# Scaling W1 behind node tiles 23 to 33, and gating edge step 0 before step 1's rows are fetched

## What is computed

```python
x = layernorm(x + L0(x))      # mean over neighbours, three 256-wide products, a gate for each node
# L1, for each of 4 heads:
feats  = relu(x @ W1 + b1) @ W2 + b2
hid    = relu(concat(feats[row], feats[col], elem) @ A1 + ab1)
w      = exp(leaky_relu(hid @ A2 + ab2) - max)
pooled = segment_sum(w * feats[col], row) / segment_sum(w, row)
x = layernorm(x + pooled)
```

## Time and profile before

| | us |
|---|---|
| median of 3 runs | 2942.45 (2941.87 to 2944.29) |
| the profiled execution, its own time | 2944.66 |
| its span, first to last instruction | 2942.9 |
| first block, until | about 27 |
| merged block, until | about 1031 |
| edge block, until | about 2630 |
| mean granted clock of PE | 0.973 |

### The profile page before, as it was taken

How to read it: one execution, slowest core, us unless ns; L and a number is a source line. 1 busy time by engine, 2 the same in 40 slices (tenths; PEclk the granted TensorE clock), 3 DMA queues, 4 the chain that set the end, 5 groups by cost and what they waited for, 6 DMA issues and landing times. The chain is left out here.

```text
span 2942.9 us, 52181 instructions
## 1 busy us (share of the span) xinstructions
PE 2697.9 (92%) x13617; PEld 1554.7 (53%) x13617; DVE 2329.0 (79%) x7668; ACT 1851.3 (63%) x3839; POOL 1582.4 (54%) x1491
## 2 busy tenths in 40 slices
PE   4789889999999959999999999999999999976774
PEld 2455556666666525555555555555555555543442
DVE  8777775655565668888888888888888888878996
ACT  2344445555555437777777777777777777757885
POOL 0476717676666375455455454454554554405776
PEclk8799999999999979999999999999999999999998
DMA  9999995565555478777777787777777777647994
GB/s 339 304 301 314 306 308 182 187 192 180 182 189 189 143 182 218 215 223 214 213 227 214 213 221 216 215 218 217 219 217 212 226 213 212 193 118 241 278 278 154
DMA packets 544632, 653.46 MB, mean 222 GB/s; under 512 B 244302, under 2 KB 451850, under 8 KB 544518
## 3 DMA queue, kind: packets, MB, share of 16 engines
q1 hardware_dynamic: 468486, 440.38, 51.6%
q0 software_dynamic: 69472, 208.99, 22.7%
q10 hardware_dynamic: 6560, 2.84, 0.4%
HBM read 315.65 MB, written 299.10 MB: 209 GB/s over the span
## 5 line engine op out<-in xcount | busy, mean ns | idle before, releaser
L942 PE MATMUL bank<-w_node,xT 128*128 128x384 f32 x1564 | 568.5, 501 | 47.2 <-ACT bank L576 46.9
L1219 ACT ACTIVATE hidT<-bank,b1c 128x512 f32<-128x512 f32 x490 | 336.8, 687 | 414.5 <-PE bank L1509 340.7
L1128 POOL TENSOR_TENSOR u_hc<-u_hc 128x1536 f32<-128x1536 f32 x98 | 270.2, 2757 | 551.0 <-issue 429.0
L1509 PE MATMUL bank<-xh,w1h 128*128 128x512 f16 x1568 | 469.8, 381 | 23.1 <-DMA xh<-eh 15.7
L1509 PE MATMUL bank<-xl,w1h 128*128 128x512 f16 x1568 | 468.2, 380 | 0.0
L1509 PE MATMUL bank<-xh,w1l 128*128 128x512 f16 x1568 | 468.2, 380 | 0.0
L942 PEld LDWEIGHTS bank<-w_node,xT 128*128 128x128 f32 x1564 | 291.4, 195 | 227.7 <-ACT bank L576 61.6
L576 ACT ACTIVATE bank<-bias_all 128x512 f32<-128x512 f32 x391 | 234.3, 599 | 267.4 <-DVE H L680 266.2
L1525 PE MATMUL bank<-hidT,w2f 128*64 128x256 f32 x3136 | 360.1, 382 | 0.8 <-ACT hidT L1219 0.8
L1350 DVE STREAM_TRANSPOSE feat<-catT 32x256 f32<-32x256 f32 x784 | 342.5, 437 | 17.0 <-ACT catT L1228 2.4
L673 DVE SCALAR_TENSOR_TENSOR H<-bank,gates,X 128x256 f32<-128x256 f32 x391 | 187.2, 479 | 175.1 <-PE bank L942 172.5
(11 more groups left out here) (248 smaller groups left out, 4833.0 us busy)
## 6 DMA issues: line engine op xcount, KB each, us to landing
hc_tab<-H SPq DMA_DIRECT2D x78, 680.0 KB, 7.9
er<-edge_tab SPq DMA_DIRECT2D x98, 512.0 KB
X<-in_x SPq DMA_DIRECT2D x78, 640.0 KB, 4.8
h_row<-hc_tab SPq DMA_DIRECT2D x97, 512.0 KB
out_x<-o_row SPq DMA_DIRECT2D x97, 512.0 KB, 5.0
hc_tab<-zero_row SPq DMA_DIRECT2D x35, 1344.0 KB, 8.4
edge_tab<-u_x SPq DMA_DIRECT2D x98, 256.0 KB
edge_tab<-feat SPq DMA_DIRECT2D x98, 256.0 KB
```

Source lines behind the costliest of these rows:

```text
L942: ins = t_.matmul(p[:, 0:384], xT[t // 2 % XR][:, t % 2, c * P:(c + 1) * P], w_node[:, c, :], start=False, stop=c == 1, skip_group_check=True)
L1128: g.tensor_tensor(c, c, u_hc[s][:, :, MULT:MULT + 3].unsqueeze(3).to_broadcast([P, 4, 3, P]), ALU.mult).then_inc(u_scaled, 1)
L1219: a.activation(hidT[m][:, :], bank[2 + m % 2][:, :], ACT.Relu, bias=b1c[:, m:m + 1])\
L1509: ins = t_.matmul(bank[2 + m % 2][:, :], w[:, c, m * P:(m + 1) * P], xx[s][:, :, :].rearrange("p (k c) e -> p c k e", c=2)[:, c, :, :], st ...
```

## The change

The eleven pieces of `scale_w1` go into the merged block. Behind tile 22 PE turns W1 (now into banks 4 to 7), behind tile 28 it spreads the powers. On DVE piece k stands behind tile 23 + k: pieces 0 to 3 one bank's maxima and minima each, 4 the powers, 5 b1 and W2, 6 and 7 the product with W1 (half the columns each), 8 the cast, 9 and 10 the subtraction, now one half of 1,024 elements each. Their buffers and semaphores are made in the merged block. In the edge block `scale_w1`, the transposes and PE's wait for `rows_read` go. On POOL the order becomes fetch 0, gate 0, fetch 1, fetch 2, gate 1, fetch 3, gate 2, and so on.

```diff
@@ merged block @@
+        SCALE = 22
@@ DVE @@
+                def scale_w1(k):
+                    if k < 4:
+                        w1_extremes(k)
+                    elif k == 4:
+                        w1_powers()
+                    elif k == 5:
+                        w2_down()
+                    elif k < 8:
+                        w1_up(k - 6)
+                    elif k == 8:
+                        w1_high()
+                    else:
+                        w1_low(k - 9)
...
+                def w1_low(c):
+                    if c == 0:
+                        st.wait()
+                    st.done(v.tensor_tensor(w1l[:, c, :], w1f[:, c, :], w1h[:, c, :], ALU.subtract))
+                    if c:
+                        st.wait()
+                        dve.sem_inc(w1_scaled, 1)
...
+                    if 0 <= now - SCALE - 1 < 11:
+                        scale_w1(now - SCALE - 1)
@@ PE @@
+                def turn_w1():
+                    pe.wait_ge(edge_sem, pc[1])
...
+                    if now == SCALE:
+                        turn_w1()
+                    if now == SCALE + 6:
+                        turn_up()
@@ edge block, POOL @@
-                skewed(pool, US, GS, [(gate, 2), (fetch, 0)])
+                fetch(0, 0)
+                gate(0, 0)
+                fetch(1, 1)
+                skewed(pool, US, GS, [(gate_rest, 2), (fetch_rest, 0)])
@@ edge block, DVE @@
-                scale_w1()
@@ edge block, PE @@
                 open_scores(0)
-                for m in range(MB):
-                    for c in range(2):
-                        o = (2 * m + c) % 4 * P
-                        ins = t_.transpose(bank[2 + m // 2][:, o:o + P], w1f[:, c, m * P:(m + 1) * P], ident[:, :])
-                ins.then_inc(w_turned, 1)
-                pe.wait_ge(up_ready, 1)
...
-                pe.wait_ge(rows_read, 4)
                 open_scores(1)
```

More of the change, by code:

```diff
@@ L391, in build @@
         o_main = out[0:P * NT].rearrange("(p t) d -> p t d", p=P)
+        MB = 2 * HEADS
+        X_UP = float(1 << 11)
+        TOP = 13
+        w_most, w_least = tmp("w_most", [P, MB]), tmp("w_least", [P, MB])
+        w_pow, w_up = tmp("w_pow", [P, MB], I32), tmp("w_up", [P, MB], I32)
+        w_down = tmp("w_down", [P, MB])
+        w_turned, up_ready, up_rows, rows_read, w1_scaled = (sem(n) for n in (
+            "w1_turned w1_up_ready w1_up_rows w1_rows_read w1_scaled").split())
         PAIRS = ET // 2
@@ new lines, in w2_down @@
+                def w2_down():
+                    dve.wait_ge(edge_sem, pc[1])
+                    dve.sem_inc(dve_hop, 1)
+                    st.done(v.scalar_tensor_tensor(out=b1c[:, :], in0=b1c[:, :], scalar=X_UP,
+                                                   in1=w_up[:, :].bitcast(F32), op0=ALU.mult, op1=ALU.mult))
+                    st.done(v.tensor_tensor(w2f[:, :, :], w2f[:, :, :],
+                                            w_down[:, :].unsqueeze(2).to_broadcast([P, MB, FEAT]), ALU.mult))
@@ new lines, in w1_up, with w1_high @@
+                def w1_up(i):
+                    dve.wait_ge(up_rows, 1)
+                    sl = slice(i * 512, (i + 1) * 512)
+                    for c in range(2):
+                        st.done(v.tensor_tensor(w1f[:, c, sl], w1f[:, c, sl], bank[4 + i][:, :], ALU.mult))
+                def w1_high():
+                    st.wait()
+                    st.done(v.tensor_copy(w1h[:, :, :], w1f[:, :, :]))
+                def w1_low(c):
+                    if c == 0:
+                        st.wait()
+                    st.done(v.tensor_tensor(w1l[:, c, :], w1f[:, c, :], w1h[:, c, :], ALU.subtract))
+                    if c:
+                        st.wait()
+                        dve.sem_inc(w1_scaled, 1)
@@ L987, in sums, with turn_up @@
                         product_sum(2 * (p - LAG_P) + 1)
+                def turn_w1():
+                    pe.wait_ge(edge_sem, pc[1])
+                    for m in range(MB):
+                        for c in range(2):
+                            o = (2 * m + c) % 4 * P
+                            ins = t_.transpose(bank[4 + m // 2][:, o:o + P], w1f[:, c, m * P:(m + 1) * P],
+                                               ident[:, :])
+                    ins.then_inc(w_turned, 1)
+                def turn_up():
+                    pe.wait_ge(up_ready, 1)
+                    for m in range(MB):
+                        o = m % 4 * P
+                        ins = t_.transpose(bank[4 + m // 4][:, o:o + P],
+                                           w_up[:, m:m + 1].bitcast(F32).to_broadcast([P, P]), ident[:, :])
+                    ins.then_inc(up_rows, 1)
                 def carries():
@@ L1062, in build @@
         ACT_M, DVE_M = (0, 2, 4, 6, 7), (1, 3, 5)
[L1063 to L1070, removed]
         hidT = [tmp(f"hidT{m}", [P, 512]) for m in range(8)]
@@ L1133, in gate, with gate_rest, fetch_rest @@
                         .then_inc(u_gated, 1)
-                skewed(pool, US, GS, [(gate, 2), (fetch, 0)])
+                def gate_rest(u, s):
+                    if not isinstance(u, int) or u > 0:
+                        gate(u, s)
+                def fetch_rest(u, s):
+                    if not isinstance(u, int) or u > 1:
+                        fetch(u, s)
+                fetch(0, 0)
+                gate(0, 0)
+                fetch(1, 1)
+                skewed(pool, US, GS, [(gate_rest, 2), (fetch_rest, 0)])
             @block.sync
```

19 lines of the change are left out of this document (added).

## The result

| | before | after |
|---|---|---|
| median of the runs | 2943.32 (16 runs) | 2949.01 (16 runs) |
| lowest to highest | 2941.87 to 2945.25 | 2945.15 to 2951.70 |
| the profiled execution, its own time | 2944.66 | 2945.15 |
| its span | 2942.9 | 2943.4 |

What follows compares the result with a forecast made beforehand. DMA was taken to bound 130 to 440 us, PE the two long stretches after. A merged-block shift of +10.5 us, handed on, and -0.5 at the edge block's start gave +10.0: median 2952.5 us, range 2941 to 2961.

Steps and rivals of the forecast that it cites:

- The pieces on DVE: Merged block: the eleven pieces of scale_w1 cost DVE 13.1 us in sum (12.5 to 14).
- The rule on the cast: Piece 8 on DVE could wait for one indirect DMA's issue, making the sum 14 us instead of 13.1.
- Transposes of W1: PE at tile 22 of the merged block: 16 transposes put 2.0 us on the path.
- The second set: PE's 8 transposes behind tile 28, when DVE is the slower engine: 0 us on the path (bound 1).
- The landing: The store after tile 34 lands 8.7 to 9.7 us after issue, so the next half shifts +9.5 to +11.4, taken +10.5.
- Does the rest come back?: DMA-bound stretch after tile 34: no, the shift, taken as +10.5 us, is handed on to the end.
- rival B: DMA stretch absorbs the delay in part through irregular DVE waits; half the shift left gives 2947 us; chance 0.20.
- The edge block: Its start: u_h of step 0 starts 5.8 us earlier, POOL idles 3.2 us, PE's steady work moves only -0.5 us.
- C: Pieces wholly hidden and step 0's 5.8 us reach the end if PE's start hangs on gate 0: 2936.7 us; chance 0.12.
- D: PE gaps from DVE's pieces lower the granted clock in two halves: +6 us more, 2958.5, up to 2964; chance 0.08.

Runs made afterwards that it cites:

- e7: Kernel before plus 8 dummy PE transposes behind every fifth node tile from 42 to 187: 2942.29 us, ratio 0.9997.
- e10: Changed kernel plus 8 dummy PE transposes behind every fifth node tile from 42 to 187: 2949.53 us, ratio 1.0021.
- the two halves alone: Changed kernel with POOL's old order: 2947.11 us; kernel before with only POOL's new order: 2945.07 us.
- the spread version: Changed kernel with one piece behind every fifth tile, POOL's old order and PE's W1 transposes behind tile 19: 2935.30 us, ratio 0.9973.

## Why the prediction was right or wrong, point by point

- **The pieces on DVE.** Reductions 0.60 apart, the product 1.28 for two, the cast 1.22, the subtraction 2 x 1.22, powers 1.2: the sum of 13.1 holds. The lengthening that `w1l` and POOL's copy showed beside each other in the earlier trace rows is gone from both (2 x 1.22 for 3.24, 0.19 for 2.25).
- **The rule on the cast.** I had weighed a rule by which the cast could wait for an indirect DMA's issue, and 14 us by it. The cast took 1.22 and had no wait: the 13.1 that I took holds. It was POOL that paid, as the timeline of POOL shows:

```profile
149.77 0.94 POOL L527 DMA_INDIRECT pay<-rec_tab,ids_at  x1 [0.31 <-issue]
151.01 1.46 POOL L527 DMA_INDIRECT pay<-rec_tab,ids_at  x1 [0.30 <-issue]
152.78 0.94 POOL L527 DMA_INDIRECT pay<-rec_tab,ids_at  x1 [0.30 <-issue]
154.03 1.69 POOL L527 DMA_INDIRECT pay<-rec_tab,ids_at  x1 [0.30 <-issue]
156.02 1.94 POOL L527 DMA_INDIRECT pay<-rec_tab,ids_at  x1 [0.30 <-issue]
```

  Issues of 0.94 us took 1.46 beside the cast at 151.13 and 1.69 and 1.94 beside the two subtractions at 153.68 and 155.93, 2.3 us in all, which POOL could spare: it later waited some 64 us before its sums. Four more profiled executions with the same pieces show the same (1.40 to 1.65, 1.68 to 1.69, 1.94). The Trainium skill, page "SBUF — State Buffer", section "Who interferes with whom", has the cast blocking descriptor writing, and here the trace agrees; of a two-input instruction it infers that it doesn't, and here the trace does not agree.
- **PE.** Transposes of W1: 1.91 for 2.0. The second set was costed at "0 (bound 1)", and this step failed: PE waited 3.8 us for the powers, then had 1.45 us to do ahead of the next node product, and DVE waited 2.1 us for that. The powers had been late behind four pieces of reductions. The node products behind the set took 4.11 us with the clock at its lower level, against 2.75 for the eight ahead of it. With this the stores stand at 131.8, 145.9 and 158.7 against 132.3, 144.6 and 157.6: +12.4 in place of +11.4.
- **The landing.** The next start of a half, 168.22, came 9.5 us behind the store at 158.67 (I had 8.7 to 9.7), so the lag there is 168.22 - 155.93 = 12.3 where I took 10.5: the missed 1.0 of the store, and a landing no quicker than before.
- **"Does the rest come back?"** I said no, since "the DMA share of 0.96 says that there is nearly no idle transfer time to catch up with". This is the step that failed. 0.04 of 310 us are 12.4 us, just as much as the shift. Half of it came back (6.2 of 12.4 by medians). In one pair of executions all but 2.4 us came back and in another 9.0 did not, and where neither of a pair had idle DMA time later on (`e7` and `e10`), 10.4 did not. So the forecast's number came out within its range by its width, and not because this step was right. That was the middle course of rival B, at 0.20, but not for its reason: DVE's waits didn't shrink (53.4 us after in 160 to 440 us, 50.0 before); what shrank was the DMA engines' idle time.
- **The edge block.** All of it held: rows landed 4.2 us after the fetch, POOL idle for 3.3 (3.2), `u_h` +8.6 (8.4), -0.5 net. That POOL idles for what the removed work gives is also what the two halves alone show. The gate's second part in step 2 stayed at 2.03.
- **The rivals.** C fell: PE's long run hangs on step 2. D, amplified by a falling clock, held in its mechanism and not in its price: in both profiled executions of the change the clock fell to 1.2 GHz between 140 and 144 us, once PE had waited 3.8 and 3.7 us. But it stood there for 3 us, not for two halves, and DVE was the slower engine by then: the store after tile 29 came 1.3 us behind the forecast, and PE's late second set has part in that too. The Trainium skill's section on gaps ("TensorE: Matmul & The Clock Gate", "HAM oscillation — how this bites in real kernels") says that gaps bring the clock down; by it the falls belong to PE's gaps, and the traces agree so far: those in the two kernels came behind gaps of 1.9 to 4.2 us, and there was none behind tile 42 in the four runs that kept PE busy from there on. But such a gap alone doesn't settle it. The second execution of the kernel before has this one, with a clock of 1.00 behind it:

```profile
354.98 2.85 PE L942 MATMUL bank<-w_node,xT 128*128 128x384 f32 x8 [2.75 <-ACT bank L576]
```

- **What stays open.** How much of the regained time is owed to the falls, and how much to other DMA idle time: the sum by shares fits one pair of executions to 0.5 us and the other to 3. Why medians gain so little from the absence of falls (1.5 us, by the interval from 3.5 us faster to 1.8 slower), when single executions show 3 to 4 us lost at one; what else makes executions of one program differ by 8 us; and why the spread version is 8.5 us faster when the edge block gives only 3.0 of it, so that the merged block with one piece a half is some 5 us shorter than without any. No run was made to tell these apart.

## What to carry to other kernels

Work that fits a bound engine's neighbour as a sum (13 us into 57 us of waits) has to fit each wait by itself: one piece of about 1.2 us a half cost nothing that a median shows, eleven pieces over three halves cost 12 us at that place. A delay in a stretch bound by DMA may be paid only in part, as far as the traces here go because the stretch had idle DMA time of its own; turn the share into microseconds over the stretch and hold it against the shift before calling it full. And an operation that is taken ahead in a queue must have its data by then: with rows that take 4.2 us to land, the fetch that stood between was the better filling.

## What the runs showed of the hardware that I had not expected

- Short falls of the granted clock in a stretch that PE fills to 0.89: behind a PE gap of 1.9 to 4.2 us the clock stands at 1.2 GHz for some 3 us, while other gaps of up to 2.75 us had no fall behind them. What is lost is more than PE's time: behind the fall at 178 us the DMA engines stand at shares of 0.12 and 0.04 for 4 us. With 8 small transposes a half from tile 42 on (PE 194 of 200 us) there was none; with 8 from tile 77 on, in the spread version (PE 190.7 of 200), one was left.
- An instruction of DVE with two inputs in SBUF stretched the issue of an indirect DMA beside it from 0.94 to 1.69 and 1.94 us, and the cast stretched one to 1.46; DVE's own times stayed at 1.22.
- Executions of one program spread over 5 to 9 us in this kernel (2937.73 to 2945.27 for the kernel before in one group of 19). In the two profiled executions of the changed kernel the spans differ by 4.6 us, and 4.4 of them are there at the last fetch of step 0, behind the stretch bound by DMA; in the two of the kernel before it is 2.5 and 2.3. Where PE was made the bound, five runs lay within 2.1 us, and five within 1.7.
